# Half of the score tiles of an attention transposed on VectorE instead of TensorE, a projection moved to the PSUM bank that this frees, and work reordered at the stage boundaries

## The reference

```python
# layer 0 (16 heads of 8 features; Wt gives six modulation vectors for each sequence)
tp = (silu(cond) @ Wt + bt)[:, None, :]
shift_msa, scale_msa, gate_msa, shift_mlp, scale_mlp, gate_mlp = split(tp, 6)
h = layernorm(x, g1, be1) * (1 + scale_msa) + shift_msa
q, k, v = heads(h @ Wqkv + bqkv)
h = softmax(q @ k.T * HD ** -0.5) @ v          # over the 32 keys of the sequence
x = x + gate_msa * (h @ Wproj + bproj)
h = layernorm(x, g2, be2) * (1 + scale_mlp) + shift_mlp
x = x + gate_mlp * (gelu(h @ W1 + b1) @ W2 + b2)
# layer 1 (one head of 128 features)
h = film(rmsnorm(x, norm1_w), cond)
x = x + softmax(Q @ K.T * D ** -0.5) @ V @ proj_w + proj_b
h = film(rmsnorm(x, norm2_w), cond)
x = x + gelu(h @ mlp_w1 + mlp_b1) @ mlp_w2 + mlp_b2
```

## Time and profile before

| what | value |
|---|---|
| median of three runs | 274.64 us (274.15, 274.64, 276.51) |
| the profiled execution's own time | 276.22 us |
| its span in the trace | 274.4 us |
| busy in the span: PE, DVE, ACT, POOL | 250.5, 163.9, 154.6, 161.4 us |
| mean granted TensorE clock | 0.994 |

### The profile page before, as it was taken

How to read it: one execution, slowest core, us unless ns; L and a number is a source line. 1 busy time by engine, 2 the same in 40 slices (tenths; PEclk the granted TensorE clock), 3 DMA queues, 4 the chain that set the end, 5 groups by cost and what they waited for, 6 DMA issues and landing times.

```text
span 274.4 us, 9959 instructions
## 1 busy us (share of the span) xinstructions
PE 250.5 (91%) x3772; PEld 188.1 (69%) x3772; DVE 163.9 (60%) x500; ACT 154.6 (56%) x340; POOL 161.4 (59%) x169
## 2 busy tenths in 40 slices
PE   0698887999999997889999999989999999999996
PEld 0556665877878876457777777857676477777775
DVE  4869864769769765354445554488889655441112
ACT  2468645668668675495555455564655655455440
POOL 6544432764864865466676666699999854345110
PEclk9999999999999998999999999999999999999999
DMA  6953332434333451450000000000000001111112
GB/s 223 317 201 85 98 104 77 121 79 125 120 91 110 110 123 40 119 153 4 0 0 0 0 0 0 2 1 5 0 0 0 0 11 32 38 38 39 38 41 76
DMA packets 17450, 18.00 MB, mean 66 GB/s; under 512 B 2320, under 2 KB 13072, under 8 KB 17296
## 3 DMA queue, kind: packets, MB, share of 16 engines
q1 hardware_dynamic: 16848, 15.67, 19.8%
q10 hardware_dynamic: 576, 1.98, 2.1%
HBM read 11.48 MB, written 4.59 MB: 59 GB/s over the span
## 4 chain that ended last, share of the span: by engine, by line
PE 70%; DVE 9%; ACT 7%; issue 7%; POOL 2%; DMA 2%; ACTq 1%; DVEq 0%; SPq 0%; POOLq 0%
PE bank L1129 21%; PE bank L943 17%; PE bank L985 6%; PE bank L998 5%; PE bank L1014 5%; PE bank L919 4%; PE bank L1036 2%; PE bank L950 2%; ACT squares L882 2%; PE bank L958 2%; ACT xhat L750 2%; PE bank L965 2%; DMA X<-x 2%; DVE smax L515 1%; DVE stats L463 1%
## 5 line engine op out<-in xcount | busy, mean ns | idle before, releaser
L750 ACT ACTIVATE xhat<-X,shift,rstd 128x128 f32 (+1 forms) x96 | 40.1, 484 | 47.1 <-POOL shift L321 47.1
L1129 PE MATMUL bank<-W,Kx 128*128 128x128 f32 x512 | 59.6, 275 | 0.0
L1129 PEld LDWEIGHTS bank<-W,Kx 128*128 128x128 f32 x512 | 58.5, 192 | 1.0 <-issue 1.0
L943 PE MATMUL bank<-h,W 128*128 128x512 f32 x124 | 56.8, 599 | 0.2 <-ACT Kx L805 0.2
L332 POOL TENSOR_TENSOR h<-hA,B 128x512 f32<-128x512 f32 x32 | 34.1, 1066 | 27.1 <-DVE hA L492 27.1
L805 ACT ACTIVATE Kx<-bank,col 128x512 f32<-128x512 f32 x64 | 39.1, 676 | 8.6 <-PE bank L943 8.6
L492 DVE TENSOR_TENSOR hA<-bank,A 128x512 f32<-128x512 f32 x32 | 21.9, 686 | 33.1 <-PE bank L919 16.8
L943 PEld LDWEIGHTS bank<-h,W 128*128 128x128 f32 x124 | 22.6, 194 | 22.5 <-issue 22.3
L340 POOL TENSOR_TENSOR Ss<-Sc,smax 128x512 f32<-128x512 f32 x16 | 16.9, 1059 | 35.4 <-DVE smax L515 35.4
L319 POOL TENSOR_TENSOR rstd<-v_sb,minus_half 128x4 f32<-128x4 f32 x24 | 24.6, 1024 | 14.6 <-DVE v_sb L483 9.2
L919 PEld LDWEIGHTS bank<-ident,xhat 128*128 128x128 f32 x128 | 15.9, 146 | 15.6 <-issue 10.5
(11 more groups left out here) (117 smaller groups left out, 391.2 us busy)
## 6 DMA issues: line engine op xcount, KB each, us to landing
values_scratch<-Vs SPq DMA_DIRECT2D x8, 288.0 KB, 2.8
Vx<-values_scratch SPq DMA_DIRECT2D x32, 72.0 KB, 2.0
gate<-gates_scratch SPq DMA_DIRECT2D x32, 64.0 KB, 2.2
gate<-gates_scratch SPq DMA_DIRECT2D x16, 128.0 KB, 2.6
out<-X SPq DMA_DIRECT2D x7, 256.0 KB, 2.3
Kx<-Ks SPq DMA_DIRECT2D x24, 64.0 KB, 1.9
W<-weights ACTq DMA_DIRECT2D x1, 1152.0 KB, 6.5
X<-x SPq DMA_DIRECT2D x4, 256.0 KB, 6.7
```

What stands on the lines that cost most here:

```text
L750: last = act.activation(xhat[:, p, P * t:P * (t + 1)], X[:, x_tile(gg, t), :], ACT.Identity, bias=shift[:, p, t:t + 1], scale=rstd[:, p, t ...
L943: last = pe.matmul(bank[2 + n][:, :], w(f"W1_{phase // 2}", n), h[:, p, :], start=True, stop=True)
L1129: last = pe.matmul(y[t // 2][:, P * t:P * (t + 1)], gT[:, p, n, P * t:P * (t + 1)], w(f"W2_{phase // 2}", n), start=(n == 0), stop=(n == N ...
```

## The change

1. The scores of a half are laid out by row tile instead of by sequence parity: even row tiles go to bank 4, odd ones to bank 5 (`odd(b)`, `in_turns`). The number and the sizes of the products are the same.
2. `scores_T` transposes only the odd row tiles, four transposes instead of eight. The even ones are turned by one VectorE instruction, a stream transpose of the sixteen 32 x 32 blocks of each 128 columns (`turn`, at the end of `shift_scores`), from `Ss` to a new tile `St`. `exps` reads `St` from SBUF in place of bank 1.
3. A transpose in blocks leaves the head index in another place than a full one. So `values0` reads the columns of its weights in another order for even tiles, and `weigh0` writes its 36 output columns for even tiles as four pieces of nine with a stride.
4. Bank 1 is free in `attention0`, so `project0` always writes there. It no longer waits for `modulate`, and `rows_T` no longer waits for `update`. `output_T(7)` goes to bank 7.
5. At the boundary to `mlp(1)`: TensorE does `up(1, 1)` chunks 0 and 1 ahead of `output_T(7)` and chunks 2 and 3 ahead of `project0(7)`; `down(1, 0)` goes ahead of `rows_T(11)`. ScalarE does `gelus` chunks 2 and 3 ahead of `move_o(7)`.
6. In `attention1`, `values1(0)` waits for the last `update` of `mlp(1)` to have read `y_ps` (`y_used`), not for GpSimd's addition behind it (`x_updated`).
7. In group 0 of `mlp(3)`, VectorE does `aggregate(27)` ahead of `modulate(26)`.

```diff
-        def slot(b):
-            return b % (GB // 2) // 2
+        def in_turns(half):
+            return [b + TB * t for b in range(half * GB // 2, half * GB // 2 + TB) for t in range(2)]
+
+        def odd(b):
+            return b // TB % 2
...
         def ot_bank(g):
-            return bank[1] if isinstance(g, int) and g == NG - 1 else bank[3]
-
-        def y0_bank(g):
-            return y_ps if isinstance(g, int) and g == NG - 1 else hT_ps
+            return bank[7] if isinstance(g, int) and g == NG - 1 else bank[3]
...
+            def turn(g, half):
+
+                hh = 2 * g + half
+                dve.wait_ge(s_shifted[0], hh + 1)
+                wait(dve, pt_ready[0], hh)
+                dve.transpose(St[:, :], Ss[:, half, 0, :]).then_inc(st_ready[0], 1)
+
             def shift_scores(g, half):
                 row_max(g, half, 0)
                 subtract_max(g, half)
                 row_max(g, half, 1)
+                turn(g, half)
...
+                    elif first:
+                        dve.wait_ge(stats_done, gg + 4 - skipped)
+                        aggregate(gg + 3, 1 - p, False, skipped)
+                        modulate(gg + 2, p)
                     elif phase < 3 or known(g, 0, 5):
                         modulate(gg + 2, p, gg + 3 - skipped)
                         aggregate(gg + 3, 1 - p, False, skipped)
...
-                for odd in range(2):
-                    act.wait_ge(st_ready[odd], hh + 1)
-                    if odd == 0:
+                for n, turned in enumerate((St, bank[7])):
+                    act.wait_ge(st_ready[n], hh + 1)
+                    if n == 0:
                         wait(act, pv_done, hh)
-                    act.activation(PT[:, odd, :], bank[1 + 6 * odd][:, :], ACT.Exp).then_inc(pt_ready[odd], 1)
+                    act.activation(PT[:, n, :], turned[:, :], ACT.Exp).then_inc(pt_ready[n], 1)
...
-                    else:
+                    gelus(m, p, (2, 3))
+                    if first and phase == 1:
                         move_o(7, 1)
-                    gelus(m, p, (2, 3))
...
-                to = bank[2][:, :].rearrange("p (r t f) -> p t r f", r=HQ, t=TG)
+                to = bank[2][:, :].rearrange("p (n t m f) -> p t n m f", n=HQ, t=TG, m=HQ)
+                by_r = w("Wqkv", 2).rearrange("p (r a f) -> p r a f", r=HQ, a=HQ)
+                by_a = w("Wqkv", 2).rearrange("p (r a f) -> p a r f", r=HQ, a=HQ)
                 for t in range(TG):
-                    last = pe.matmul(to[:, t], h[:, p, P * t:P * (t + 1)], w("Wqkv", 2), start=True, stop=True)
+                    last = pe.matmul(to[:, t], h[:, p, P * t:P * (t + 1)], by_r if t % 2 else by_a, start=True, stop=True)
...
-                for odd in range(2):
-                    pe.wait_ge(s_shifted[odd], hh + 1)
-                    wait(pe, pt_ready[odd], hh)
-                    for n in range(GB // 4):
-                        at = slice(P * n, P * (n + 1))
-                        last = pe.transpose(bank[1 + 6 * odd][:, at], Ss[:, half, odd, at], ident[:, :])
-                    last.then_inc(st_ready[odd], 1)
+                pe.wait_ge(s_shifted[1], hh + 1)
+                wait(pe, pt_ready[1], hh)
+                for n in range(GB // 4):
+                    at = slice(P * n, P * (n + 1))
+                    last = pe.transpose(bank[7][:, at], Ss[:, half, 1, at], ident[:, :])
+                last.then_inc(st_ready[1], 1)
...
+                even_o = bank[6][:, 0:OW].rearrange("p (a r f) -> p r a f", a=HQ, r=HQ)
+                odd_o = bank[6][:, OW:2 * OW].rearrange("p (a r f) -> p a r f", a=HQ, r=HQ)
...
+                        from_ = P * (b % TB) + (rows_at(b, n) if odd(b) else L * n)
+                        to = (odd_o if odd(b) else even_o)[at:at + L, n]
+                        last = pe.matmul(to, PT[:, odd(b), from_:from_ + L],
+                                         Vx[:, p, :, at_v(b, n):at_v(b, n) + VW], start=True, stop=True)
...
             def project0(g, p):
                 pe.wait_ge(ot_moved, g + 1)
-                if not (isinstance(g, int) and g == NG - 1):
-                    pe.wait_ge(hA_ready, g + 4)
+                pe.wait_ge(y_used, g + 1)
                 for t in range(TG):
-                    last = pe.matmul(y0_bank(g)[:, P * t:P * (t + 1)], OTs[:, p, P * t:P * (t + 1)], w("Wproj"),
+                    last = pe.matmul(y_ps[:, P * t:P * (t + 1)], OTs[:, p, P * t:P * (t + 1)], w("Wproj"),
...
                     if first:
                         pe.wait_ge(rows_ready, 1)
-                    else:
-                        pe.wait_ge(y_used, g + 1)
                     rows_T(g + 3, 1 - p)
...
-                pe.wait_ge(x_updated, 2 * NG + g + 1)
+                if isinstance(g, int) and g == 0:
+                    pe.wait_ge(y_used, 2 * NG + 1)
+                else:
+                    pe.wait_ge(x_updated, 2 * NG + g + 1)
...
                     if first and phase == 1:
+                        pe.wait_ge(ot_moved, NG - 1)
+                        up(1, 1, 1, (0, 1))
                         output_T(7, 1)
-                        pe.wait_ge(y_used, NG)
...
-                        up(1, 1, 1, (0, 1))
+                        up(1, 1, 1, (2, 3))
                         project0(7, 1)
-                        up(1, 1, 1, (2, 3))
+                    if phase == 1 and isinstance(g, int) and g == 1:
+                        down(1, 0, 0)
+                        rows_T(gg + 2, p)
+                        return
```

More of the change, by code:

```diff
@@ L500, in update @@
                     dve.wait_ge(x_updated, gg + 1)
[L501 to L502 removed]
+                    dve.tensor_tensor(by_tile(yG[:, :]), by_tile(y_ps[:, :]), biases(phase), ALU.add).then_inc(y_used, 1)
                 else:
@@ L980, in scores0 @@
             def scores0(p, half):
-                for b in of_half(half):
+                for b in in_turns(half):
                     for a in range(HQ):
                         rows_of, at = slice(L * a, L * (a + 1)), rows_at(b, a)
-                        last = pe.matmul(bank[4 + b % 2][at:at + L, P * slot(b):P * (slot(b) + 1)],
+                        last = pe.matmul(bank[4 + odd(b)][at:at + L, P * (b % TB):P * (b % TB + 1)],
                                          Qs[rows_of, p, L * b:L * (b + 1)], Kx[rows_of, p, :, L * b:L * (b + 1)],
@@ L992, in scores_T @@
                 hh = 2 * g + half
[L993 to L999 removed]
+                pe.wait_ge(s_shifted[1], hh + 1)
[4 more added lines that the diff above has]
+                last.then_inc(st_ready[1], 1)
             def weigh0(g, p, half, following=None):
                 hh = 2 * g + half
[L1004 to L1005 removed]
+                for n in range(2):
+                    pe.wait_ge(pt_ready[n], hh + 1)
                 wait(pe, o_used, hh)
[L1007 to L1008 removed]
+                even_o = bank[6][:, 0:OW].rearrange("p (a r f) -> p r a f", a=HQ, r=HQ)
+                odd_o = bank[6][:, OW:2 * OW].rearrange("p (a r f) -> p a r f", a=HQ, r=HQ)
+                for n in range(HQ):
+                    if n == HQ - 1 and following is not None:
                         wait_scores(*following)
@@ L1011, in weigh0 @@
                         at = L * (b % TB)
-                        to = b // TB % 2 * OW + a * HQ * VW
-                        from_ = P * slot(b) + rows_at(b, a)
-                        last = pe.matmul(bank[6][at:at + L, to:to + HQ * VW], PT[:, b % 2, from_:from_ + L],
-                                         Vx[:, p, :, at_v(b, a):at_v(b, a) + VW], start=True, stop=True)
+                        from_ = P * (b % TB) + (rows_at(b, n) if odd(b) else L * n)
+                        to = (odd_o if odd(b) else even_o)[at:at + L, n]
+                        last = pe.matmul(to, PT[:, odd(b), from_:from_ + L],
+                                         Vx[:, p, :, at_v(b, n):at_v(b, n) + VW], start=True, stop=True)
                 last.then_inc(pv_done, 1)
```

16 lines of the change are left out of this document (5 added, 11 removed).

## The result

The changed kernel takes 273.92 us (median of 20 executions, 271.11 to 276.32), the kernel before 274.99 (20, from 273.63 up, one of them 423.42) beside it. The ratio is 0.9933, 95% interval [0.9906, 0.9959]: 0.7% faster, where 2.9% was forecast. Medians here are over all executions, while ratios and their intervals leave out the executions more than 1.5% above the fastest of their kernel, so that a ratio is not the quotient of the two medians. The profiled execution took 273.66 us, span 271.8.

What follows compares the result with a forecast made beforehand. TensorE's own work bounds `attention0` from group 1; it waits in group 0 and at boundaries. From 276.22 us, +1.1 - 5.3 - 3.4 - 0.4 = -8.0 gives 268.2, as a median 266.8; range 264.3 to 271.8.

Steps and rivals of the forecast that it cites:

- the boundary to `mlp(1)`: `down(1, 0)` starts at 117.8 instead of 121.24: gain 3.4 us, 0.5 of it the transposes; bounds 1.5 and 3.8.
- Rival (b): Boundary to `mlp(1)` gives only 0.5 us, another wait taking the place of the one removed: 269.5 us; chance 0.08.
- Group 0: Start of `attention0`: VectorE's three turns make `rows_ready` 1.7 us later; loss 0.6 to 1.7, taken as 1.1.
- the first stop: Group 0, TensorE's 1.12 us stop inside `scores0`, looking like instruction loading: loss 0.6 if swallowed by the wait, otherwise 1.7.
- second stop: Group 0, TensorE's 1.95 us stop inside `scores0`, for no cause the profile names; looks like instructions being loaded.
- The six groups: Groups 1 to 6 of `attention0`: 9.5 us each instead of 10.39, gain 0.89 a group, 5.3 for six.
- The walk: One `attention0` group traced through all engines at 9.4 us: all waits met, none with more than a microsecond to spare.
- rival (c): `weigh0` in `attention0`: strided writes take double, +0.96 us a group over six, some 272.5 us; chance 0.06.
- rival (d): VectorE's stream transpose costs by blocks; kernel slower from 1.17 us each, 275.8 us at 1.25; chance 0.06.
- VectorE over 95% busy: Sign of being right: groups of 9.4 to 9.6 us between 50 and 97 us, VectorE over 95% busy.
- the 0.6 us that should arrive: Start of `attention1`: TensorE 1.0 us earlier, of which some 0.6 arrives at the stage's end, GpSimd giving the pace.
- The second: Boundary to `mlp(3)`, `aggregate` ahead of `modulate`: `power(27)` between 0.4 us earlier and 0.2 later.

Runs made afterwards that it cites:

- fold_agg_power: Changed kernel, group 0's folded weights made first, and group 1 of `mlp(1)` written out with `aggregate(12)` and `power(12)` ahead of `modulate(11)` and `add_shift(11)`: 268.93 us, 0.9767.
- turns_fold: Changed kernel with the later boundaries in their old order (transposes and freed bank only) and group 0's folded weights made first on VectorE: 270.49 us, 0.9834.
- boundaries_only: Kernel before with only the new order at the boundaries to `mlp(1)`, `attention1` and `mlp(3)`, no transposes moved: 276.95 us, 1.0075.
- fold_first: Changed kernel with VectorE making group 0's folded weights ahead of shifting and turning half 0 of group 1: 272.35 us, 0.9882 of the kernel before.

## Why the prediction was wrong

The forecast was 266.8 us with a range from 264.3 to 271.8; 273.92 lies above the whole range.

**The step that failed is the boundary to `mlp(1)`**, in its sentence on what is late next. It listed `normalise(7)`, the gelus, `apply(10)` and GpSimd's addition for group 10, and ended with "It holds by 0.6" for `up(1, 2)`. All of these held, and from `scores_T` of group 7 to `down(1, 0)` 3.0 us were won of the 3.4 forecast (18.61 to 15.61; a wait of 0.44 for `update` is left ahead of it). Missing is what stands behind `rows_T(11)`, which the change puts behind `down(1, 0)`: `modulate(11)`, `aggregate(12)`, `add_shift(11)`, `power(12)`, `apply(12)`, `rows_T(12)`. For the instructions that went forward the prediction asked who waits for what is queued behind them, and for `rows_T(11)`, which went back, it didn't. The forecast gain of 3.4 us had 0.5 of the transposes and 2.9 of the order. The order lost 1.0 to 1.2 instead. With the two engines' order mended, the stretch from `scores_T` of group 7 to `down(1, 1)` is 23.55 us in `fold_agg_power`, against 25.61 in `turns_fold` with the old order: 2.1 of the 2.9. Rival (b) had the mechanism, another wait in the place of the one removed, with a gain of 0.5 as its price instead of a loss.

**Group 0** was forecast at a loss of 1.1 and came to 1.34 at `scores_T` of group 1 in the profile, by other terms. Right were the 1.7 us at `rows_T(3)`. Wrong was the choice between two values for the first stop. The prediction would have it swallowed if the load runs on while TensorE waits; at full clock the stop stays at 0.82 to 1.40 us, whether the wait ahead is 1.95 or 0.57. Where it is all but gone, as in the profiled execution, the clock is low ahead of it, and the low clock was not in the forecast. The prediction set beside this a rule of the Trainium skill's page Runtime: NRT & Kernel Launch, section Instruction fetch mechanics, by which a taken branch outside the loaded pages forces a fetch, and read from it that the load begins no sooner for a wait. The stops at full clock agree with that reading; that they are fetches at all, no run here shows. At `scores_T` of group 2 the changed kernel is 0.09 us behind, where 1.1 - 0.89 = 0.2 was forecast. That is luck: the low clock and the shorter second stop, neither of them forecast, cancel.

**The six groups** gave 4.42 us (65.46 to 61.04, from `scores_T` of group 1 to that of group 7) where 5.3 was forecast. By group, from 1 to 6, it is 1.25, 0.72, 0.06, 0.81, 0.83 and 0.75, where each was to give 0.89. One term was mis-sized: four transposes alone take 0.59 us, not half of 1.02, so a half saves 0.43 and a group 0.86. The forecast had taken 0.13 for losses off its 1.02, so that with 0.86 in place of 0.89 its sum over six groups changes by 0.2 only. The row is in the chain of the changed kernel:

```profile
64.77 0.59 PE bank L1010 x4
65.35 0.89 PE bank L1049 x8
```

Most of the rest is group 3, which lost 0.74 to K's transfer. The walk had no transfers in it. The 1.25 of group 1 has the shorter second stop in it, 0.93 us, and is luck as far as that goes. The hand-overs between the engines cost about 0.1 us or less in groups 4 to 6. Strides: `weigh0` takes 200 ns a product by line in both kernels, as many in a group and as long in all (1.9 us), and rival (c) falls. The transpose took 704 ns against 708, rival (d) falls. The sign "VectorE over 95% busy" didn't come true: it is 91 to 94%.

**`attention1` and `mlp(3)`**: the wait became 0.34 as forecast, but the 0.6 us that should arrive was 0. GpSimd's pace takes all of it: its `scale_rows` of the next group starts at 180.73 instead of 183.32, 2.59 us earlier, no more than the 2.60 with which the stage began. The second was nothing, inside its bounds.

In sum the profile shows -2.6 where -8.0 was forecast: 3.9 of the 5.4 are the boundary (26.06 us from `scores_T` of group 7 to `down(1, 1)` before and 26.53 after, where 3.4 less was forecast), 0.9 the six groups, 0.2 group 0, 0.4 what lies behind.

## What to carry to other kernels

When an instruction is moved ahead of another, follow the one that was passed over just as far: list what other engines do only after it, in their queue's order, up to the next instruction of the first engine. A gain at the moved instruction is not a gain until the next one of its kind comes earlier too; compare two successive ones (here `down(1, 0)` and `down(1, 1)`). And where a step is measured as a run of eight, half of it is not its price for four.

## What the runs showed of the chip

After a wait of 1.95 us TensorE's clock was down to half for about 3 us in four of eight profiled kernels, and after one of 0.57 us in none of four. After the wait of 1.88 to 2.31 us for exponentials at the boundary it was low in twelve of fourteen. What such a stretch costs depends on what TensorE has to do in it: 1.9 us between `boundaries_only` and the kernel before at the boundary (20.24 and 22.16 us of busy time for the same work), 1.6 in `down(1, 1)` of `fold_first`, but 0.3 to 1.0 behind `rows_T(3)`, where a stop of about 1 us follows that is gone or short after a low stretch. The mean clock of each execution, which stands beside its time, counts the stretches; a table of times by clock separates this part of the scatter from the change. Another part is a store whose landing took 2.2 to 2.3 us in two profiled kernels and 3.6 to 4.8 in the other twelve, with the loads queued behind it.
